# Patch planes on other partitions, and images one behind the other with 64-channel row tiles

## What is computed

```python
x = x + L0_conv(gn(x))   # gn: 32 groups of 2 neighbouring channels
x = x + L1_conv(gn(x))
# L0: 3x3 convolution of sign(x) with sign(weight), times a scale per channel
# L1: r = relu(batchnorm(w_r @ x))            64 -> 16 channels, pointwise
#     ker = w_s @ r                           16 -> 49 taps x 16 groups, at every point
#     out[group, d] = sum over the 7x7 taps of x_shifted[group, d] * ker[group, tap]
```

## Time and profile before

| | |
|---|---|
| median of three runs | 2026.53 us |
| profiled execution | 2020.96 us |
| its span, first to last instruction | 2019.1 us |
| mean granted TensorE clock | 0.925 |
| TensorE busy (matmul) | 1658.4 us, 82% |
| VectorE busy | 1380.2 us, 68% |
| ScalarE busy | 1058.4 us, 52% |
| GpSimd busy | 1024.6 us, 51% |
| moved by DMA | 436.41 MB, mean 216 GB/s |

### The profile page before, as it was taken

How to read it: one execution, slowest core, us unless ns; L and a number is a source line. 1 busy time by engine, 2 the same in 40 slices (tenths; PEclk the granted TensorE clock), 3 DMA queues, 4 the chain that set the end, 5 groups by cost and what they waited for, 6 DMA issues and landing times.

```text
span 2019.1 us, 39160 instructions
## 1 busy us (share of the span) xinstructions
PE 1658.4 (82%) x15072; PEld 751.8 (37%) x15072; DVE 1380.2 (68%) x1700; ACT 1058.4 (52%) x758; POOL 1024.6 (51%) x905
## 2 busy tenths in 40 slices
PE   3588897879788798897879888797887978978785
PEld 1243343333343343343433343343333433334342
DVE  5476776858577685776758677585776757768574
ACT  2364565546555554565545555454555545655453
POOL 2155465545455555455545545454555454645574
PEclk8799998989899899998989999898998989989898
DMA  4679899897989989899897998979899897998894
GB/s 104 169 196 241 202 250 231 211 240 191 239 208 255 219 201 240 205 244 227 209 229 194 235 221 228 231 195 246 204 252 222 206 226 198 247 229 220 199 268 110
DMA packets 224139, 436.41 MB, mean 216 GB/s; under 512 B 89198, under 2 KB 136607, under 8 KB 219807
## 3 DMA queue, kind: packets, MB, share of 16 engines
q1 hardware_dynamic: 148688, 382.51, 76.6%
q10 hardware_dynamic: 75264, 51.39, 10.2%
HBM read 335.99 MB, written 84.93 MB: 208 GB/s over the span
## 4 chain that ended last, share of the span: by engine, by line
POOL 46%; issue 43%; SPq 2%; DVE 2%; DMA 2%; PE 2%; ACT 1%; POOLq 1%; ACTq 0%; DVEq 0%
POOL folded L365 46%; SPq L304 1%; SPq L286 1%; PE ybank L569 1%; DMA back<-consts_dram 1%; DMA parts_dram<-parts 1%; POOLq L364 0%; DMA patches<-parts_dram 0%; DVE prod L791 0%; PE ybank L550 0%; DVE bn L753 0%; ACT patches L432 0%; SPq L294 0%; DVE xs L749 0%; SPq L255 0%
## 5 line engine op out<-in xcount | busy, mean ns | idle before, releaser
L365 POOL TENSOR_TENSOR folded<-prod 128x448 f32<-128x448 f32 x896 | 1012.9, 1143 | 972.6 <-DVE prod L791 971.8
L791 DVE TENSOR_TENSOR prod<-ybank,relu 128x896 f32<-128x896 f32 x896 | 961.1, 1088 | 432.3 <-PE ybank L569 383.9
L569 PE MATMUL ybank<-patches,wspan 128*64 128x448 f16 x7168 | 857.5, 380 | 232.0 <-DMA patches<-parts_dram 113.7
L432 ACT ACTIVATE patches<-patches 64x1792 f16<-64x1792 f16 x448 | 741.8, 1700 | 553.7 <-DMA patches<-parts_dram 298.0
L569 PEld LDWEIGHTS ybank<-patches,wspan 128*64 128x64 f16 x7168 | 394.0, 116 | 740.8 <-issue 409.1
L511 PE MATMUL ybank<-sgn,convw 128*128 128x448 bf16 x1008 | 205.2, 357 | 23.8 <-ACT sgn L385 19.4
L587 PE MATMUL obank<-folded,esum 128*32 128x448 f32 x1792 | 214.8, 551 | 1.5 <-POOL folded L365 1.5
L580 PE MATMUL obank<-patches,wbias 128*32 128x448 f16 x3584 | 197.1, 363 | 0.0
L511 PEld LDWEIGHTS ybank<-sgn,convw 128*128 128x128 bf16 x1008 | 93.3, 97 | 136.9 <-issue 33.1
L782 DVE TENSOR_TENSOR parts<-ybank,parts 128x1024 f16<-128x1024 f32 x64 | 79.5, 1243 | 74.9 <-ACT parts L404 74.7
L580 PEld LDWEIGHTS obank<-patches,wbias 128*32 128x32 f16 x3584 | 87.2, 98 | 103.6 <-issue 49.9
(11 more groups left out here) (91 smaller groups left out, 411.9 us busy)
## 6 DMA issues: line engine op xcount, KB each, us to landing
patches<-parts_dram SPq DMA_DIRECT2D x1232, 224.0 KB, 7.4
parts_dram<-parts SPq DMA_DIRECT2D x128, 256.0 KB, 7.5
xs<-x_dram SPq DMA_DIRECT2D x128, 196.0 KB, 6.0
sums_dram<-osb ACTq DMA_DIRECT2D x112, 224.0 KB, 6.6
rows<-sums_dram ACTq DMA_DIRECT2D x112, 224.0 KB, 6.8
out_dram<-xs SPq DMA_DIRECT2D x128, 196.0 KB, 3.8
relu<-blocks SPq DMA_DIRECT2D x256, 49.0 KB
patches<-gb_dram SPq DMA_DIRECT2D x1, 784.0 KB
```

Source lines behind the costliest of these rows:

```text
L365: pool.tensor_tensor(folded[:, u % 8, :], prod[:, u % 2, 0, :], prod[:, u % 2, 1, :], ALU.add).then_inc(fold_done, 1)
L432: act.activation(X2[0:COPIED_ROWS, e % 2, at], X1[0:COPIED_ROWS, e % 3, at], ACT.Copy).then_inc(copied, 1)
L569: mm = pe.matmul(bank("unit", p, n)[64 * t:64 * t + 64, h, 0:N], wspan[0:STACK_ROWS[stack], stack, g, h, :], of_group(e, stack, g), start= ...
L791: dve.tensor_tensor(prod[:, u % 2].rearrange("m h (n c) -> m h n c", c=GC), bank("unit", p, n)[:, :, 0:N].rearrange("m h (n c) -> m h n c" ...
```

## The change

It has two parts, with small ones that go with them.

**Planes.** Each plane of the first stack moves to other rows. Four of the eight now lie in partitions 32 to 95, every fourth row (32, 36, ... 92 for the first); the other four lie in partitions 0 to 31 or 96 to 127, every second row. The planes that the second stack shares with the first are now five planes' rows, 0 to 95, copied by the same four ScalarE instructions with 96 partitions instead of 64. The second stack fetches two planes instead of three. All rows of X2 are written, so its clearing at the start is gone. The loads and stores of xs use the same pattern of rows, 8 transfers of 16 rows as before.

**Images.** Partition 64b + ch now holds channel ch of image b. `reduce` reads, for image b, only its 64 partitions and a weight of 64 rows and 32 columns, and the loops are swapped, dy outside and b inside. `ident` becomes a permutation that restores the old order in the transposed data; the blocks V are laid out so that `outputs` gives the new order, and the `arrange` instruction therefore writes runs of 4 elements instead of 8.

```diff
+ROWS16 = tuple(slice(*r) for i in range(2) for r in ((32 + 2 * i, 96, 4), (i, 32, 2), (33 + 2 * i, 96, 4), (96 + i, 128, 2)))
-PLANES = (((0, 0, 0, 4), (0, 4, 64, 4), (0, 1, 1, 4), (1, 0, 65, 4),
-           (0, 2, 2, 4), (1, 1, 66, 4), (0, 3, 3, 4), (1, 2, 67, 4)),
-          tuple((0, a, a, 4) for a in range(4)) + ((0, 4, 64, 4), (1, 3, 65, 4), (1, 4, 66, 4)))
-COPIED_ROWS, COPIED_PLANES = 64, 4
+PLANES = (((0, 0, 32, 4), (0, 4, 0, 2), (0, 1, 33, 4), (1, 0, 96, 2),
+           (0, 2, 34, 4), (1, 1, 1, 2), (0, 3, 35, 4), (1, 2, 97, 2)),
+          ((0, 0, 32, 4), (0, 4, 0, 2), (0, 1, 33, 4), (0, 2, 34, 4), (0, 3, 35, 4),
+           (1, 3, 96, 2), (1, 4, 97, 2)))
+COPIED_ROWS, COPIED_PLANES = 96, 5
...
-FIRSTLOAD, SECONDLOAD = 16 * 8, 16 * 3
+FIRSTLOAD, SECONDLOAD = 16 * 8, 16 * 2
...
-                for b in range(2):
-                    for c in range(GC):
-                        sp.dma_start(xs[4 * b + c:128:8, p % 3, :], xv[p][b][c]).then_inc(x_loaded, 16)
+                for rows in ROWS16:
+                    sp.dma_start(xs[rows, p % 3, :], xv[p][rows]).then_inc(x_loaded, 16)
...
-            pool.memset(X2[:].rearrange("p a n -> p (a n)").bitcast(U32), 0).then_inc(zeroed, 1)
...
-                act.activation(V[0:rows].rearrange("m y g n -> m g y n"), U[0:rows], ACT.Copy).then_inc(arranged, 1)
+                act.activation(V[0:rows].rearrange("m y b g c -> m g y b c"),
+                               U[0:rows].rearrange("m g y (b c) -> m g y b c", b=2), ACT.Copy).then_inc(arranged, 1)
...
-                for b in range(2):
-                    for dy in range(PY):
+                for dy in range(PY):
+                    for b in range(2):
                         cy, yp = (dy + PAD) // 2, (dy + PAD) % 2
-                        rhs = xn4[:, cy:cy + 2 * JY - 1:2, k + PAD:k + PAD + W - 1:2, yp].rearrange("p y x -> p x y")
-                        mm = pe.matmul(bank("red", p, k)[32 * dy:32 * dy + 32, b, 0:HW // POS], wred[:, b, :], rhs,
+                        rhs = xn4[C * b:C * (b + 1), cy:cy + 2 * JY - 1:2, k + PAD:k + PAD + W - 1:2, yp].rearrange("p y x -> p x y")
+                        mm = pe.matmul(bank("red", p, k)[32 * dy:32 * dy + 32, b, 0:HW // POS], wred[C * b:C * (b + 1), :], rhs,
                                        start=True, stop=True)
...
-    c[:, C_ID:C_ID + 128] = np.eye(128)
+        c[m, C_ID + 8 * (m % C // GC) + GC * (m // C) + m % GC] = 1
```

More of the change, by code:

```diff
@@ L62 @@
 P_N = P_CONV + 9 * C
-FIRST_LOADS, LOADS, ZEROS = 16 * 2, 16 * 6, 5
+FIRST_LOADS, LOADS, ZEROS = 16 * 2, 16 * 6, 4
 XLOAD, STORE = 16 * 8, 16 * 8
-FIRSTLOAD, SECONDLOAD = 16 * 8, 16 * 3
+FIRSTLOAD, SECONDLOAD = 16 * 8, 16 * 2
 COPY = JY * 128
@@ L105, in build @@
 def build(nc, x, consts, params, span, gb_all, out, pairs=PAIRS):
-    xv = x.rearrange("(p b) (g c) h w -> p b c g (h w)", b=2, c=GC)
-    ov = out.rearrange("(p b) (g c) h w -> p b c g (h w)", b=2, c=GC)
+    xv = x.rearrange("(p b) c h w -> p (b c) (h w)", b=2)
+    ov = out.rearrange("(p b) c h w -> p (b c) (h w)", b=2)
     TURNS = turns(pairs)
@@ L132, in build @@
         U = sb("rows", [128, GROUPS, JY, 8])
-        V = sb("blocks", [128, JY, GROUPS, 8])
-        rsum = V[:].rearrange("p y g n -> p (y g n)")[:, 0:PX * 2 * HW // POS].rearrange("p (x n) -> p x n", x=PX)
+        V = sb("blocks", [128, JY, 2, GROUPS, GC])
+        rsum = V[:].rearrange("p y b g c -> p (y b g c)")[:, 0:PX * 2 * HW // POS].rearrange("p (x n) -> p x n", x=PX)
         ident = sb("ident", [128, 128])
@@ L138, in build @@
         convw = sb("convw", [128, 9, 128], BF16)
-        wred = sb("wred", [128, 2, 32])
+        wred = sb("wred", [128, 32])
         mask = sb("mask", [128, 2])
@@ L252, in load @@
             def load(p):
-                for b in range(2):
-                    for c in range(GC):
-                        sp.dma_start(xs[4 * b + c:128:8, p % 3, :], xv[p][b][c]).then_inc(x_loaded, 16)
+                for rows in ROWS16:
+                    sp.dma_start(xs[rows, p % 3, :], xv[p][rows]).then_inc(x_loaded, 16)
             def store(p):
                 sp.wait_ge(out_added, 4 * (p + 1))
-                for b in range(2):
-                    for c in range(GC):
-                        sp.dma_start(ov[p][b][c], xs[4 * b + c:128:8, p % 3, :]).then_inc(stored, 16)
+                for rows in ROWS16:
+                    sp.dma_start(ov[p][rows], xs[rows, p % 3, :]).then_inc(stored, 16)
             def parts_out(p, k):
@@ L358, in _ @@
             pool.memset(wbias[:].rearrange("p a b c -> p (a b c)").bitcast(U32), 0).then_inc(zeroed, 1)
-            pool.memset(wred[:].rearrange("p a b -> p (a b)").bitcast(U32), 0).then_inc(zeroed, 1)
-            pool.memset(X2[:].rearrange("p a n -> p (a n)").bitcast(U32), 0).then_inc(zeroed, 1)
+            pool.memset(wred[:].bitcast(U32), 0).then_inc(zeroed, 1)
             for u in range(UNITS * pairs):
@@ L371, in _ @@
             for b in range(2):
-                act.activation(convw[:].rearrange("p t (g b c) -> p t g b c", b=2, c=GC)[:, :, :, b, :],
-                               t_par[:, P_CONV:P_N].rearrange("p (t g c) -> p t g c", t=9, c=GC),
+                act.activation(convw[:, :, C * b:C * (b + 1)],
+                               t_par[:, P_CONV:P_N].rearrange("p (t c) -> p t c", t=9),
                                ACT.Sign, scale=mask[:, b:b + 1]).then_inc(convw_ready, 1)
@@ L555, in of_group @@
                 at = (X1[:, e % 3, :], X2[:, e % 2, :])[stack]
-                return at[0:STACK_ROWS[stack]].rearrange("k (j g n) -> k g j n", g=GROUPS, n=8)[:, g]
+                return at.rearrange("k (j g n) -> k g j n", g=GROUPS, n=8)[:, g]
             def taps(p, n):
@@ L569, in taps @@
                             mm = pe.matmul(bank("unit", p, n)[64 * t:64 * t + 64, h, 0:N],
-                                           wspan[0:STACK_ROWS[stack], stack, g, h, :], of_group(e, stack, g),
+                                           wspan[:, stack, g, h, :], of_group(e, stack, g),
                                            start=(stack == 0), stop=(stack == 1))
@@ L579, in bias @@
                         g = 4 * t + i
-                        pe.matmul(Obank[e % 2][32 * t:32 * t + 32, 0:N], wbias[0:STACK_ROWS[stack], stack, g, :],
+                        pe.matmul(Obank[e % 2][32 * t:32 * t + 32, 0:N], wbias[:, stack, g, :],
                                   of_group(e, stack, g), start=(stack == 0 and i == 0), stop=False)
@@ L601, in outputs @@
                         mm = pe.transpose(bank("out", p, k)[:, i, rows * n:rows * (n + 1)],
-                                          V[0:rows, by].rearrange("m g n -> m (g n)"), back[0:rows, group, 0:rows])
+                                          V[0:rows, by].rearrange("m b g c -> m (b g c)"), back[0:rows, group, 0:rows])
                 mm.then_inc(out_ready, 1)
@@ L698, in setup @@
                 split(t_b16[:, 0, :], t_b16[:, 1, :], t_b)
-                for b in range(2):
-                    link(dve.tensor_scalar(wred[:, b, 0:O], t_par[:, P_VT:P_VT + O], mask[:, b:b + 1], None, ALU.mult))
+                link(dve.tensor_copy(wred[:, 0:O], t_par[:, P_VT:P_VT + O]))
                 def par(i):
@@ L863, in constants @@
         c[m, C_E + 16 + 8 * (m // 64) + 2 * (m % 64 // 16) + m % 2] = 1
-        c[m, C_M + m // 4 % 2] = 1
+        c[m, C_M + m // C] = 1
+        c[m, C_ID + 8 * (m % C // GC) + GC * (m // C) + m % GC] = 1
     for group, width in enumerate((32, 24)):
@@ L873, in layouts @@
     import numpy as np
-    at = np.array([4 * (m // 8) + m % 4 for m in range(128)])
+    at = np.arange(128) % C
     p = np.zeros((128, P_N), np.float32)
```

2 lines of the change are left out of this document (removed).

## The result

The changed kernel takes 1969.74 us (median of 4, 1965.92 to 1978.51), the kernel before in the same comparison 2023.04 us: ratio 0.9749, interval 0.9721 to 0.9778. That is 53 us where 153 were forecast. The direction was right and the size was not. The measured median lies just inside the edge of the stated range (1790 to 1970), which is the range's width and no merit of the sum.

What follows compares the result with a forecast made beforehand. TensorE was taken to work nearly all the time, with some 17 us of gaps per pair and transfers almost as full. Terms 47 + 27 + 45 + 13 + 30 + 6 - 15 = 153 us off 2021 gave 1870 us, range 1790 to 1970.

Steps and rivals of the forecast that it cites:

- Points 3 and 4: TensorE's waits: transposes late behind copies, 27 us gained (0 to 32); two copy waits per pair, 45 us (0 to 60).
- Point 6: TensorE's clock: fewer dips to half rate after gaps, 30 us gained, from 0 to 45.
- point 1: DMA queues: 2.2 us less transfer time per step, 17 of 108 us per pair with loads and stores; no time by itself.
- Point 2: Reduction on TensorE: row halves side by side, a group of 16 in 1.58 instead of 3.03 us, 47 us gained.
- Point 5: Wait behind spread stays; one transfer less to issue and two planes instead of three give 13 us, from 9 to 25.
- Point 7: Start and end: planes and pair 0 arrive sooner, about 6 us gained, from 0 to 12.
- Point 8: Costs nothing: copies of 96 partitions, `arrange` in runs of 4, the permutation and the order of V; taken as 0.
- Point 9: Given back once gaps are gone: VectorE at pair starts and GpSimd's fold set some units, 15 us, from 0 to 50.
- Neither part does anything: Rival: neither the planes nor the images part gains, 2010 us; chance 0.03.
- The halves make no difference: Rival: something other than row position holds planes to 240 GB/s; 97 us gained, 1924 us; chance 0.17.
- Row tiles take turns: Rival: the reduction's two images can't overlap, 7.4 us instead of 3.03 per group, 2055 us; chance 0.08.
- outer planes get slower: Rival: outer planes' rows in 32 neighbouring partitions, at twice 0.96 us each, make the queues the limit, near 2170 us; chance 0.05.

## Were the gaps what the forecast took them for?

From the fourth step on this kernel leaves out four of the eight planes of the first stack, and the rows meant for them keep old data, so its result is not the reference's.

```diff
-                for l, a, row, step in PLANES[0]:
+                for l, a, row, step in PLANES[0][0:(8 if e < 3 else 4)]:
-                                 plane(e, l, a)).then_inc(first_in[e % 3], 16)
+                                 plane(e, l, a)).then_inc(first_in[e % 3], 16 if e < 3 else 32)
```

> The changed kernel, but from the fourth step on only four of the eight planes of the first stack are fetched (the other rows keep old data, so the result is not the reference's). It shows what faster transfers would have been worth. If points 3, 4 and 6 of the forecast were right about the gaps and only the rate was off: the copies' wait for planes falls from 307 to under 100 us, TensorE's waits for copies from 71 to under 15 us, and the time to 1870 to 1900. Rival (the gaps come back as other waits even with fast transfers): 1940 to 1970. The wait behind the spread stays at 6 to 7 us in both.

Measured: 1865.21 us, ratio 0.9211 (0.9185 to 0.9236), 105 us below the changed kernel. Its waits:

```profile
ACT patches L432 <- DMA patches<-parts_dram: 142.2, 32, 12.9
PE ybank L571 <- DMA patches<-parts_dram: 96.4, 16, 7.0
...
PE ybank L571 <- ACT patches L432: 23.8, 2, 20.3
```

TensorE's waits for copies are gone but for the start's 20.3 us, its wait for VectorE's split is gone from the list, and the wait behind the spread stays with 6.0 us a time. The copies' own wait for planes fell to 142.2 us, not to under 100, and the time is 5 us below the band. So the chain from planes to copies to taps was read rightly, and less transfer work pays. Two limits: the edit also halves the issues of SP for the first stack, so it doesn't tell time in the queues from time to issue. And it took 445 us of queue time away (1467 to 0.549 x 1861.9 = 1022 us) for 105 us, while the forecast hoped for 102 us in points 3, 4 and 6 from 17 x 16 = 272 us. The first thing that failed lies before the chain, in the rate; whether the chain would have paid 102 us for 272 is not shown.

## What a transfer's rows do to its rate

Stretches of transfers alone were put behind the last store of the changed kernel, eleven kinds in one run and seven in another. Each was run once.

> The changed kernel, and behind its last store eleven stretches of transfers alone, issued by ScalarE, one kind each: planes onto rows 0 to 60 by 4, onto 32 to 92 by 4, onto 0 to 30 by 2; the same bytes as 64 rows of 3584 bytes and as 128 rows; x onto 16 rows in one half, onto 16 rows in the middle, onto all 128; xs to DRAM from 16 rows in one half, in the middle, in one quarter. If the rows on the SBUF side set the rate (the forecast): 240 GB/s, then 330 to 370 in the middle, then 240. If the one-row-per-queue shape sets it, whatever the rows: 240 for all 16-row fetches, 330 and more for 64 and 128 rows. If the reading of DRAM sets it: about 240 for every fetch, also with 128 rows, and more only for the writes to DRAM.

The stretches, with the columns of the earlier trace rows (the last two are DMA share and GB/s). In order: planes on rows 0 to 60 by 4; on 32 to 92 by 4 (two rows); on 0 to 30 by 2; 64 rows; 128 rows; x onto 16 rows of one half; of the middle; onto 128; then to DRAM from one half, the middle, one quarter.

```profile
1968.00:1970.00 2.00, 0.00 (x0) 0.00 (x0) 0.00 (x0) 0.00 (x0) 0.00 (x0) 0.50 1.02 208
...
1980.00:1982.00 2.00, 0.00 (x0) 0.00 (x0) 0.00 (x0) 0.00 (x0) 0.00 (x0) 0.50 0.99 269
1982.00:1984.00 2.00, 0.00 (x0) 0.00 (x0) 0.00 (x0) 0.00 (x0) 0.00 (x0) 0.50 0.95 247
...
1992.00:1994.00 2.00, 0.00 (x0) 0.00 (x0) 0.00 (x0) 0.00 (x0) 0.00 (x0) 0.50 1.06 212
...
2006.00:2008.00 2.00, 0.00 (x0) 0.00 (x0) 0.00 (x0) 0.00 (x0) 0.00 (x0) 0.50 1.04 208
...
2018.00:2020.00 2.00, 0.00 (x0) 0.00 (x0) 0.00 (x0) 0.00 (x0) 0.00 (x0) 0.50 0.97 332
...
2028.00:2030.00 2.00, 0.00 (x0) 0.00 (x0) 0.00 (x0) 0.00 (x0) 0.00 (x0) 0.50 1.03 213
...
2034.00:2036.00 2.00, 0.00 (x0) 0.00 (x0) 0.00 (x0) 0.00 (x0) 0.00 (x0) 0.50 0.97 307
...
2042.00:2044.00 2.00, 0.00 (x0) 0.00 (x0) 0.00 (x0) 0.00 (x0) 0.00 (x0) 0.50 0.95 395
...
2050.00:2052.00 2.00, 0.00 (x0) 0.00 (x0) 0.00 (x0) 0.00 (x0) 0.00 (x0) 0.50 0.95 201
...
2060.00:2062.00 2.00, 0.00 (x0) 0.00 (x0) 0.00 (x0) 0.00 (x0) 0.00 (x0) 0.50 0.73 301
...
2066.00:2068.00 2.00, 0.00 (x0) 0.00 (x0) 0.00 (x0) 0.00 (x0) 0.00 (x0) 0.50 0.99 201
```

For a full share: 200 to 212 GB/s in these rows wherever the partitions lie in one half, be they 16, 64 or a quarter's; all of these lie in the lower half, the upper was not run alone (the first 2 us of a stretch, not shown, can be faster, 220/0.84 = 262 in the first kind, and the share reads up to 1.06 in a full queue, so a few per cent between two kinds mean nothing). From the middle into SBUF it is 260 to 317, for planes 295 over their whole stretch, less than the 350 that the forecast took, and out of it 412 (301/0.73). With 128 rows it is 342 for planes' bytes and 416 for x. So the rows do set the rate, as the forecast had it. And yet the planes of the kernel before, each in one half, made 247 to 261. The next run shows that they do so when they come in turn, low half, high half:

> The changed kernel, and behind its last store seven stretches of plane fetches alone, 224 KB each, issued by ScalarE: half and half in turn as the first stack of before; middle and outer quarters in turn as the first stack of the change; middle only; outer quarters in turn (first, last); rows 7 apart; rows 8 apart; 16 neighbouring rows. Theory A (alternating halves already overlapped before, and the middle planes share their halves with the outer ones, so a mixed queue gains nothing): about 240 GB/s for a full share for both mixtures, 290 to 300 for middle only, 200 to 240 for the outer quarters in turn, 240 to 300 for 7 apart, 200 for 8 apart, 100 to 120 for neighbours. Rival (the mixture of the change is faster alone, and only the other traffic in the kernel hides it): 240 for the mixture of before, 270 or more for that of the change.

In order: low and high half in turn (the order of before); middle and outer quarters in turn (the order of the change); middle only; outer quarters in turn; 7 rows apart; 8 rows apart; 16 neighbouring rows.

```profile
1974.00:1980.00 6.00, 0.00 (x0) 0.00 (x0) 0.00 (x0) 0.00 (x0) 0.00 (x0) 0.50 1.03 270
1986.00:1992.00 6.00, 0.00 (x0) 0.00 (x0) 0.00 (x0) 0.00 (x0) 0.00 (x0) 0.50 1.05 235
2000.00:2002.00 2.00, 0.00 (x0) 0.00 (x0) 0.00 (x0) 0.00 (x0) 0.00 (x0) 0.50 1.01 305
2010.00:2014.00 4.00, 0.00 (x0) 0.00 (x0) 0.00 (x0) 0.00 (x0) 0.00 (x0) 0.50 1.01 237
2022.00:2026.00 4.00, 0.00 (x0) 0.00 (x0) 0.00 (x0) 0.00 (x0) 0.00 (x0) 0.50 0.94 281
2040.00:2044.00 4.00, 0.00 (x0) 0.00 (x0) 0.00 (x0) 0.00 (x0) 0.00 (x0) 0.50 1.06 209
2056.00:2062.00 6.00, 0.00 (x0) 0.00 (x0) 0.00 (x0) 0.00 (x0) 0.00 (x0) 0.50 1.06 125
```

The old order makes 262 GB/s, the new one 224, no more than the outer quarters alone (235), though half of its planes could go at 300. Over the whole stretches, with their starts, the three are 269, 242 and 239. By the rows shown, a step's fetches were 11 x 229 KB / 262 = 9.6 us before and 10 x 229 / 224 = 10.2 us after; by the whole stretches 9.4 and 9.5. Inside the kernels the two orders are alike. At the start, where planes move alone, the first line is the kernel before and the second the changed one:

```profile
70.00:76.00 6.00, 0.00 (x0) 0.00 (x0) 0.00 (x0) 0.00 (x0) 0.00 (x0) 0.55 1.00 257
70.00:76.00 6.00, 0.00 (x0) 0.00 (x0) 0.00 (x0) 0.00 (x0) 0.00 (x0) 0.50 0.99 253
```

With the rest of the traffic it is 247 and 243. The gain of the middle planes is gone there too. The rival of this run, 270 or more for the mixture of the change, fell. Theory A held in that the change's mixture gains nothing, though it took both mixtures for about equal. Its reason, that a middle plane shares its half with the outer one next to it, fits all stretches, but no run shows what the two wait for.

One more line bears on the change: rows 8 apart lie in both halves and yet make 209/1.06 = 197 GB/s. These are the rows of the loads and stores before. So reaching both halves is not enough; it matters which rows.

Sixteen neighbouring rows made 125/1.06 = 118 GB/s, the slowest of all kinds. Twelve planes in turn between the halves made 262, against 204 (208/1.02, in the run before this one) for planes in the lower half alone, 28% more.

## Four predictions from the order and the rows

The copies and the taps wait for all eight planes of a step, so the order within the eight doesn't change what they wait for; it can act through the transfers only.

**Kernel before, four low planes, then four high ones.**

```diff
-PLANES = (((0, 0, 0, 4), (0, 4, 64, 4), (0, 1, 1, 4), (1, 0, 65, 4),
-           (0, 2, 2, 4), (1, 1, 66, 4), (0, 3, 3, 4), (1, 2, 67, 4)),
+PLANES = (((0, 0, 0, 4), (0, 1, 1, 4), (0, 2, 2, 4), (0, 3, 3, 4),
+           (0, 4, 64, 4), (1, 0, 65, 4), (1, 1, 66, 4), (1, 2, 67, 4)),
```

> The kernel before with nothing changed but the order in which SP issues the eight planes of the first stack: the four of partitions 0 to 63 first, then the four of 64 to 127, instead of in turn. Theory (two transfers in opposite halves overlap in part, 262 GB/s in turn, 205 for one half alone): the planes go at 205 to 215, 2 us more per step, and the time rises by 40 to 70 us, 2060 to 2095. Rival (the order of transfers doesn't matter inside the kernel, where the queue mixes them anyway): within 0.5% of before.

Measured: 2080.3 us, ratio 1.0291 (1.0246 to 1.0337). Held.

**Changed kernel, four middle planes, then four outer ones.**

```diff
+PLANES = (((0, 0, 32, 4), (0, 1, 33, 4), (0, 2, 34, 4), (0, 3, 35, 4),
+           (0, 4, 0, 2), (1, 0, 96, 2), (1, 1, 1, 2), (1, 2, 97, 2)),
```

> The changed kernel, with only the order of the first stack's planes changed: the four middle ones first, then the four in the outer quarters. Alone, middle planes made 297 GB/s, outer ones 235, the two in turn 232. Theory (a middle plane loses its advantage next to an outer one): 4 x 0.77 + 6 x 0.98 = 9.0 instead of 9.9 us of transfers per step, and by the 105 us that four planes (3.9 us per step) were worth, some 24 us less: 1940 to 1955. Rival: no difference, 1962 to 1978.

Measured: 1939.25 us, ratio 0.9593 (0.9553 to 0.9633), 31 us below the changed kernel and just below the band.

**Halves and quarters in turn.**

```diff
+PLANES = (((0, 0, 0, 4), (0, 4, 64, 2), (0, 1, 1, 4), (1, 0, 65, 2),
+           (0, 2, 2, 4), (1, 1, 96, 2), (0, 3, 3, 4), (1, 2, 97, 2)), ...
```

> The changed kernel with another place for the planes that keeps both sides: four in partitions 0 to 63, every fourth row, in turn with four in 64 to 95 and 96 to 127, every second row; five are still copied (rows 0 to 95) and two fetched. Theory (transfers in turn between the halves make about 260 as before, so the dropped plane counts at last): 10 planes in 8.8 to 9.2 us per step, 1945 to 1958. Rival (every second row, two neighbouring queues on one group of rows, is what is slow, not the mixing): 1965 to 1985.

Measured: 1953.99 us, ratio 0.9663 (0.9607 to 0.9719). Held.

**Planes alone again, middle ones first.**

> The planes on their new rows in the kernel before, the four middle ones issued first; the images and the reduction as before. In turn this part gave 12 us. Theory (the order alone gives it 30 us more): 1975 to 1990. Rival (the order gains only where the reduction is short): 1995 to 2010.

Measured: 1974.98 us, ratio 0.9772 (0.974 to 0.9803), against 0.9942 in turn. It is at the lower edge of the band. So the order alone decides whether this part is worth 14 us or 49 by the medians.

The queue rows of the first three of these kernels, with spans of 2077.7, 1938.6 and 1956.5 us:

```profile
q1 hardware_dynamic: 148688, 382.51, 81.0%
```
```profile
q1 hardware_dynamic: 139728, 356.81, 69.6%
```
```profile
q1 hardware_dynamic: 139728, 356.81, 72.4%
```

They give 227, 264 and 252 GB/s. In queue time they are 1683, 1349 and 1417 us; against their own base (1547 before, 1467 after) +136, -118 and -50 us of transfers made +58, -31 and -15 us of time. A microsecond of transfers was worth a quarter to four tenths of one. At that price the 272 us of the forecast would have given 70 to 115 us.

## Gap behind the spread, and the best version

relu's result goes to DRAM in one transfer, has its own buffer, and comes back in eight transfers that SP issues behind the planes of the next two steps. Two waits of ScalarE that the shared buffer needed go with it. (The comments in the cut below are added.)

```diff
-                        spread(p + 1)
+                        spread_out(p + 1)   # wait for relu, one transfer rsum -> DRAM
...
+                    if s == 5 and p + 1 < pairs:      # behind second_stack, first_stack
+                        spread_in(p + 1)    # wait for it, eight transfers DRAM -> R
```

> The changed kernel with the spread taken out of the way of the planes: relu's result goes to DRAM in one transfer as soon as it is there, then SP issues the second stack of the last step and the first stack of the next, and only then eight transfers that bring the result back to R; it has a buffer of its own. Theory: the wait of TensorE behind the spread (110 us, 15 times) is an issue queue, so it falls to under 20 us, and the time falls by 60 to 110 us, to 1860 to 1910. Rival (the planes behind it are late anyway, so that the same wait comes back at the copies): TensorE's waits for copies and planes together stay above 150 us and the time is 1940 to 1970.

Measured: 1958.13 us, ratio 0.9704 (0.9667 to 0.9741), only 0.5% below the changed kernel. Its waits (the profiled execution, at 1932.75 us, was the fastest of five):

```profile
ACT patches L439 <- DMA patches<-parts_dram: 373.8, 58, 12.7
...
PE ybank L577 <- ACT patches L439: 116.3, 31, 20.4
...
PE ybank L577 <- DMA patches<-parts_dram: 51.0, 15, 5.8
```

The gap behind the spread went from 110 to 51 us, not to under 20, and the copies' wait for planes grew by 67 us, TensorE's for copies by 25: two fifths of what the gap lost came back there. That fits planes that no longer wait behind the spread in SP and wait in the transfers instead, which was not tested apart. My theory fell and the rival held: the time is in its band, and the two waits together are 51.0 + 116.3 = 167 us (147 without the 20.4 us of the start).

With shorter transfers it should pay. The same, with the middle planes first, and the eight loads and stores of xs in that order:

> The changed kernel with three edits together: the middle planes ahead of the outer ones (1939 us alone), the same order for the eight loads and stores of xs, and the spread by DRAM (10 us less than the changed kernel alone, with the transfers then the limit). Theory (the transfers are the limit, so what each edit frees adds up): 1900 to 1930 us. Rival (both free the same stretch of a pair): 1930 to 1945.

Measured: 1877.58 us (1867.32 to 1882.15), ratio 0.9288 (0.9262 to 0.9315), faster than both kernels and below the band. Clock 0.939, and:

```profile
ACT patches L439 <- DMA patches<-parts_dram: 310.7, 58, 12.0
PE ybank L577 <- ACT patches L439: 93.6, 29, 19.7
PE ybank L577 <- DMA patches<-parts_dram: 47.6, 18, 4.7
```

It is 92 us below the changed kernel, where the middle planes first gave 31 and the spread by DRAM 12 when run alone. The 49 us between may come from the two together or from the order of loads and stores, which was not run alone.

## Why the prediction was wrong, step by step

- **The transfers' speed, and point 1: this step failed.** The forecast took 240 as the rate of a transfer in one half, and so 0.96 us for each outer plane and 0.66 us for each middle one. But 240 was the rate of a queue of both halves in turn; one half alone makes about 205. The old order was already using both. In the new order a middle plane next to an outer one brings no gain, and all ten go at 0.94 (243 GB/s) to 1.02 us (224). Of 2.2 us of relief per step 80/112 = 0.7 us is left, loads and stores included. The 350 for a middle plane was too high as well: 295 alone, 0.78 us instead of 0.66. The figures of the rows were copied rightly; what they stood for was not, a mixture taken for one kind. A sign stood in the trace, for the row of 209 GB/s (1010 to 1012) was not one of planes in turn:

```profile
1002.04 4.99 SPq L255 DMA_DIRECT2D xs<-x_dram  x8
1007.13 2.82 SPq L294 DMA_DIRECT2D patches<-parts_dram  x3
```

  Issued just before it were eight loads with rows 8 apart, which make 197 alone as planes, and three planes all in the upper half, the kind that makes 204 in the lower.
- **Point 2, the reduction: right.** Busy time of its records 57.8 instead of 101.2 us, 43 of 47 us; 1.8 us for a group where 1.58 was expected, so 0.1 to 0.35 us of each is more than the two turns and the lead. "Both lie on TensorE's path" was too simple: alone they gave 28 us, as the gap behind the spread grew.
- **Points 3 and 4: right as a chain, nothing arrived to drive it.** 20.1 us instead of 5 for the transposes, and 91.5 - 20.0 = 71.5 us instead of 15 for the copies (60.2 before). With four planes fewer the latter fell to 3.5 us and the former left the list.
- **Point 5**: 7.4 us per pair after 7.6; 6.5 to 7 was expected. From the last issue of the spread to the taps it is 5.0 us instead of 6.0, so the 0.9 us came; but the 16 issues took 12.6 us instead of 12.1, which leaves some 0.3 us by which TensorE reached the gap sooner.
- **Point 6**: no gain, since the gaps stayed: 0.922 after 0.925, where 0.95 or more was forecast; with shorter gaps 0.939 in the best version. Where the forecast says half rate, the granted clock in the trace before was 0.65 over the 4.90 us (0.50 from 1058 to 1060) and 1.00 over the 3.22 us.
- **Point 7**: nothing, the longest wait at the start is 20.0 instead of 18.3 us. **Point 8**: right, copies of 96 partitions take 1689 ns, and `arrange` with runs of 4 still 1690. **Point 9**: nothing of the 15 us shows; TensorE's small waits for VectorE are 33.7 us after 35.4, and 42.3 with four planes fewer.
- **Rivals.** "Neither part does anything" (2010) and "The halves make no difference" (1924) came nearest in time to 1970, both for a wrong reason: both parts do something, and the halves matter. "Row tiles take turns" is refuted by 1.8 us. That outer planes get slower was given 0.05 with a threshold of 1.6 us; alone they took 229/235 = 0.98 us, close to the 0.96 of the forecast and far below that. No rival said that the mixed order cancels the gain of the middle planes.

## What to carry to other kernels

Before a transfer is moved, ask what the queue as a whole does with both halves of the partitions: a rate read from a mixed queue need not be that of one transfer alone (here 262 GB/s in turn, 204 for one half, about 300 for the middle). Measure the order too, since the same planes in another order moved this kernel by 1.6 to 2.9%. And a wait at the head of an in-order issue queue can come back behind it, as two fifths of 59 us did here: taking it away gave 0.5% with the slow order and, together with the order of loads and stores, 3.1% with the fast one.

## What the runs showed of the hardware

- Rows 32 to 92 by 4 leave SBUF at 412 GB/s and enter it at 260 to 317; rows within the lower half make 200 to 212 either way. Rows 8 apart, over all 128, enter at 197 only.
- Middle planes in turn with quarter ones (224 GB/s in the steady part, 242 over the stretch) are no faster than quarter ones alone (235 and 239), while middle ones alone make about 300. Why the mixture loses their gain was not settled.
- Transfers with rows 7 apart, which no plane uses here, made 281/0.94 = 299 GB/s at first and 229/0.84 = 273 over their stretch.
- Float32 matmuls of 64 rows by 32 columns overlap in eight tiles: a record takes 0.90 us, 16 of them 1.7 to 1.9 us, and 1.7 to 2.0 us in the other order of loops (one run).
